# Time mixing on one Trainium2 core: three GpSimd products on VectorE, and the layer norm of batches 1 to 3 on ScalarE

## What is computed

```python
x = x + _time_mixing(_layernorm(x))
x = x + _ffn(_layernorm(x))
```

```python
p = jnp.maximum(pp, u + k);   e1, e2 = jnp.exp(pp - p), jnp.exp(u + k - p)
y = (e1 * aa + e2 * v) / (e1 * bb + e2)
p2 = jnp.maximum(pp + w, k);  e1, e2 = jnp.exp(pp + w - p2), jnp.exp(k - p2)
aa, bb, pp = e1 * aa + e2 * v, e1 * bb + e2, p2
out = (sigmoid(r) * y) @ W_out.T
```

## Time and profile before

| what | value |
|---|---|
| runs, median of 3 (lowest, highest) | 1751.03 us (1748.39, 1753.09) |
| the profiled execution's own time | 1743.46 us |
| its span, first to last instruction | 1741.7 us |
| busy in the span: PE, DVE, ACT, POOL | 92%, 83%, 64%, 61% |
| mean granted TensorE clock | 0.973 |

### The profile page before, as it was taken

How to read it: one execution, slowest core, us unless ns; L and a number is a source line. 1 busy time by engine, 2 the same in 40 slices (tenths; PEclk the granted TensorE clock), 3 DMA queues, 4 the chain that set the end, 5 groups by cost and what they waited for, 6 DMA issues and landing times.

```text
span 1741.7 us, 75944 instructions
## 1 busy us (share of the span) xinstructions
PE 1595.3 (92%) x32157; PEld 1274.2 (73%) x32157; DVE 1448.0 (83%) x3173; ACT 1116.3 (64%) x2014; POOL 1070.8 (61%) x1040
## 2 busy tenths in 40 slices
PE   5469999999999999999999999999999999999985
PEld 2247877777877777777777777777787777877863
DVE  8979988888888888879888888888889888888851
ACT  4346666676676666667667666666666666766652
POOL 3556766756766666666665766566567476575530
PEclk7689999999999999999999999999999999999997
DMA  2011110211110201111211111211111211011010
GB/s 85 31 44 48 40 49 24 76 37 35 44 49 24 76 24 48 43 36 37 60 40 48 31 49 32 59 35 50 41 36 40 61 36 48 26 46 52 28 42 13
DMA packets 41079, 74.97 MB, mean 43 GB/s; under 512 B 9472, under 2 KB 22568, under 8 KB 40744
## 3 DMA queue, kind: packets, MB, share of 16 engines
q1 hardware_dynamic: 40744, 70.12, 13.9%
HBM read 20.08 MB, written 2.10 MB: 13 GB/s over the span
## 4 chain that ended last, share of the span: by engine, by line
PE 73%; issue 9%; DVE 7%; ACT 4%; POOL 3%; ACTq 0%; DVEq 0%; POOLq 0%
PE bank L1350 8%; PE bank L1384 8%; PE bank L1453 8%; PE bank L1319 8%; PE wide L1424 7%; PE bank L1321 6%; PE bank L1320 6%; PE bank L1439 4%; PE bank L1508 4%; PE bank L1402 3%; PE bank L1374 2%; PE bank L1496 2%; PE bank L1498 2%; PE bank L1497 2%; POOL qk L847 1%
## 5 line engine op out<-in xcount | busy, mean ns | idle before, releaser
L855 POOL TENSOR_TENSOR qk<-qk,rnorm 128x512 f32<-128x512 f32 x384 | 401.7, 1046 | 347.8 <-DVE rnorm L1008 347.8
L847 POOL TENSOR_TENSOR qk<-qk,qk_sin 128x512 f32<-128x512 f32 x384 | 492.4, 1282 | 174.4 <-DVE qk_sin L969 174.3
L1171 ACT ACTIVATE squares<-bank 128x512 f32<-128x512 f32 x384 | 229.5, 598 | 154.0 <-DVE qk_sin L969 153.9
L979 DVE TENSOR_REDUCE norm<-squares 128x8 f32<-128x512 f32 x384 | 258.5, 678 | 30.7 <-ACT squares L1171 28.5
L1319 PE MATMUL bank<-w_hi,xs_hi 128*128 128x512 f32 x576 | 262.5, 456 | 13.0 <-ACT squares L1171 6.8
L962 DVE TENSOR_TENSOR qk<-bank,tables 128x512 f32<-128x512 f32 x384 | 261.7, 681 | 8.9 <-PE bank L1321 8.6
L969 DVE TENSOR_TENSOR qk_sin<-bank,tables 128x512 f32<-128x512 f32 x384 | 261.2, 680 | 0.6 <-POOL qk L847 0.6
L1321 PE MATMUL bank<-w_hi,xs_lo 128*128 128x512 f32 x576 | 229.6, 399 | 0.0
L1350 PE MATMUL bank<-ident,qk 128*128 128x128 f32 x1536 | 226.7, 278 | 2.8 <-POOL qk L855 1.7
L1320 PE MATMUL bank<-w_lo,xs_hi 128*128 128x512 f32 x576 | 228.4, 396 | 0.0
L1350 PEld LDWEIGHTS bank<-ident,qk 128*128 128x128 f32 x1536 | 180.9, 142 | 42.0 <-issue 2.8
(11 more groups left out here) (177 smaller groups left out, 2749.1 us busy)
## 6 DMA issues: line engine op xcount, KB each, us to landing
v<-v SPq DMA_DIRECT2D x96, 390.0 KB, 3.5
v<-v SPq DMA_DIRECT2D x72, 130.0 KB, 3.6
w_raw<-in_L_ffn_Wqkv SPq DMA_DIRECT2D x36, 256.0 KB, 3.8
w_o_s<-in_L_ffn_Wo SPq DMA_DIRECT2D x6, 512.0 KB, 5.9
w_raw<-in_L_ffn_W SPq DMA_DIRECT2D x6, 341.0 KB, 4.7
mix_x_nat<-in_L_attn_x SPq DMA_DIRECT2D x4, 256.0 KB, 3.5
w_raw<-x_res_scratch SPq DMA_DIRECT2D x4, 256.0 KB, 4.0
out<-w_raw SPq DMA_DIRECT2D x4, 256.0 KB, 3.3
```

The costliest lines, as they stand in the source:

```text
L847: pool.tensor_tensor(qk[:, g % 2, c, :], qk[:, g % 2, c, :], qk_sin[:, (QK_CHUNKS * g + c) % SINES, :], ALU.add).then_inc(added[c], 1)
L855: pool.tensor_tensor(view, view, rnorm[:, g % 2, c * HPC:(c + 1) * HPC].unsqueeze(2) .to_broadcast([P, HPC, DH]), ALU.mult).then_inc(norme ...
L979: dve.tensor_reduce(norm2[:, c * HPC:(c + 1) * HPC], squares[:, c % 2, :].rearrange("p (h d) -> p h d", d=DH), AX.X, ALU.add).then_inc(sum ...
```

## The change

`numerator` leaves POOL. Its three operations stand in DVE's `weigh_output`, between the operations that were there, so that no operation follows directly on the one it depends on. POOL's loop now waits for the finished denominator of batch b (den2_ready), then splits chunk 2 + b, then does newton(b - 1). The layer norm of batches 1 to 3 leaves DVE: DVE makes one more small tile, offset = -mean * rstd (128x12), and ACT writes xn as rstd * x + offset, four operations of 128x128 for a batch, with both factors read per partition from SBUF. That of batch 1 stands behind exponentials(0), that of b + 2 at the head of ACT's loop. Batch 0's stays on DVE.

```diff
-            def numerator(b):
...
             for b in range(BATCH):
-                numerator(b)
+                pool.wait_ge(den2_ready, b + 1)
                 weights.split(pool, 0, 2 + b)
                 newton(b - 1)
...
                 dve.wait_ge(f2_ready, b + 1)
+                dve.wait_ge(v_evac, b + 1)
+                dve.tensor_tensor(f2v[:], f2[:, p], v_s[:, p], ALU.mult).then_inc(f2v_ready, 1)
                 dve.wait_ge(f1b_ready, b + 1)
                 dve.tensor_tensor(den[:], f1b[:], f2[:, p], ALU.add).then_inc(den_ready, 1)
+                dve.wait_ge(aa_ready, b + 1)
+                dve.tensor_tensor(f1a[:], f1[:, p], aa[:, p, 0:SEQ], ALU.mult).then_inc(f1a_ready, 1)
                 dve.wait_ge(er_ready, b + 1)
                 dve.wait_ge(den_ready, b + 1)
                 dve.scalar_tensor_tensor(den[:], er[:, p], 1.0, den[:], ALU.add, ALU.mult).then_inc(den2_ready, 1)
+                dve.wait_ge(f1a_ready, b + 1)
+                dve.wait_ge(f2v_ready, b + 1)
+                dve.tensor_tensor(num[:], f1a[:], f2v[:], ALU.add).then_inc(num_ready, 1)
...
             spread(NBLK, BATCH * NBLK)
-            layer_norm(1)
+            dve.scalar_tensor_tensor(offset[:, NBLK:], mv[:, NBLK:, 0], -1.0, rstd[:, NBLK:], ALU.mult,
+                                     ALU.mult).then_inc(xn_ready, 1)
             for b in range(BATCH):
...
                 scan_maximum(b + 1)
-                layer_norm(b + 2)
                 weigh_output(b)
...
+            def layer_norm(b):
+                if not real(b):
+                    return
+                act.wait_ge(xn_ready, NBLK + 1)
+                for j in range(b * NBLK, (b + 1) * NBLK):
+                    act.activation(xn[:, j, :], x_nat[:, j, :], ACT.Identity, bias=offset[:, j:j + 1],
+                                   scale=rstd[:, j:j + 1]).then_inc(xn_ready, 1)
...
             exponentials(0)
+            layer_norm(1)
             take_x(1)
...
             for b in range(BATCH):
+                layer_norm(b + 2)
                 take_centred(b - 1)
```

More of the change, by code:

```diff
@@ L223, in time_mixing @@
         var, rstd, root_s, root_w = (sb(name, [P, BATCH * NBLK]) for name in ("var", "rstd", "root_s", "root_w"))
+        offset = sb("offset", [P, BATCH * NBLK])
         var2, rstd2, nt2 = (sb(name, [P, 2, NBLK]) for name in ("var2", "rstd2", "nt2"))
@@ L321, in newton @@
                 pool.tensor_tensor(y, s, y, ALU.mult).then_inc(rs_ready, 1)
-            def numerator(b):
-                p = b % 2
-                pool.wait_ge(f2_ready, b + 1)
-                pool.wait_ge(v_evac, b + 1)
-                pool.tensor_tensor(f2v[:], f2[:, p], v_s[:, p], ALU.mult).then_inc(f2v_ready, 1)
-                pool.wait_ge(f1_ready, b + 1)
-                pool.wait_ge(aa_ready, b + 1)
-                pool.tensor_tensor(f1a[:], f1[:, p], aa[:, p, 0:SEQ], ALU.mult).then_inc(f1a_ready, 1)
-                pool.wait_ge(f1a_ready, b + 1)
-                pool.wait_ge(f2v_ready, b + 1)
-                need(pool, rwkv_ready, b)
-                pool.tensor_tensor(num[:], f1a[:], f2v[:], ALU.add).then_inc(num_ready, 1)
             for c in range(2):
@@ L378, in layer_norm @@
             def layer_norm(b):
-                if not real(b):
-                    return
                 for j in range(b * NBLK, (b + 1) * NBLK):
@@ L580, in turn_x @@
                     return
-                pe.wait_ge(xn_ready, 4 * b + 4)
+                pe.wait_ge(xn_ready, NBLK * (b + 1) + (b > 0))
                 need(pe, xt_evac, 2 * b - 1)
```

## The result

| | kernel before | changed kernel |
|---|---|---|
| median of 6 runs each, us | 1750.47 (1748.39 to 1758.67) | 1740.32 (1738.88 to 1746.60) |
| ratio to before, 95% interval | | 0.9942 [0.9917, 0.9967] |
| profiled execution, us | 1743.46 | 1739.93 |
| its span, us | 1741.7 | 1737.8 |
| first DVE operation of the second block | 87.23 | 84.74 |

The median is 0.58% lower, outside the predicted range of 1743.5 to 1754. The first block ended 2.49 us earlier (forecast: 1.96). The median fell by 10.15 us, four times that. So there are two questions: where the 2.5 us came from, and where the rest did.

A forecast was written before the change was run, and what follows sets the result against it. DVE's queue was taken to bound turns 1 and 2, ACT and PE the start of turn 1, other engines the end. Terms +1.54, -1.57, -2.12, -0.84, +1.03 sum to -1.96: 1751.03 to 1749.0 us, range 1743.5 to 1754.

The forecast's parts named there:

- the base: Whole kernel: the difference is added to the median of the runs, 1751.03 us, not to the profiled execution, 1743.46.
- the sum: First block: +1.54 - 1.57 - 2.12 - 0.84 + 1.03 = -1.96 us.
- signs of being wrong: residual(0) before 42, scale_state waiting for the widening in turns 2 or 3, or second block's length moving over a microsecond.
- The second block starts that much earlier and is the same code: Second block: starts 1.96 us earlier with unchanged code, so the whole kernel gains that much.
- Start to residual(0): Block's start up to residual(0): ACT's four operations ahead of exponentials(1) cost 1.68, factors come 0.14 earlier; 1.54 us later.
- ACT's price: Rival, ACT's new layer-norm operations: 0.72 apart instead of 0.42 gives 1751.5, chance 0.10; 0.16 apart gives 1747.0, chance 0.05.
- The rival on PE's clock: Batch 2's projections: earlier transposes find PE at full level, path up to 3.15 us shorter, 1745.9; chance 0.15.
- Turns 1 to 3: residual(0) to batch 1's reciprocal -1.57; reciprocal to residual, batches 1 and 2, -2.12; residual(1) to batch 2's reciprocal -0.84.
- I cost it at nothing; the spare half microsecond is the cover: Reciprocal to residual: late newton plus widening take about 7.5 us, done before scale_state some 8 us behind num; no cost.
- The end: residual(2) to the block's end: newton follows the split at 6.85 instead of 5.82; 1.03 us later.
- The interleaving hides nothing: Rival, weigh_output's six operations: 0.78 apart like dependent ones, turns 1 to 3 pay 3.24, total 1752.3; chance 0.08.
- e2v: DVE product between reciprocal and residual, blocked by POOL's f2v: 1.75 us falls to 0.69, 1.06 less, twice.

The follow-up runs named there:

- newton first: Against the changed kernel, POOL's last turn runs newton(2) ahead of the wait and the split; 1739.11 us (1 run), second block at 82.83.
- layer norm alone: Against the kernel before, only the layer norm of batches 1 to 3 moves to ACT, products stay on POOL; 1743.61 us, ratio 0.9993.
- split at once: Against the changed kernel, POOL's wait for the denominator is removed; 1736.34 us (1 run), second block at 87.12.
- in a row: Against the changed kernel, weigh_output's six operations reordered so num, den and den2 directly follow what they need; 1751.81 us (1 run).

## Why the prediction was wrong, and where it was right

**The step that failed is the base, not the sum.** The prediction saw that the profiled execution "lies 7.57 us, 0.43%, under the median of the runs, 1751.03", and said "so I add the difference to the median". It took the scatter of three runs, "2.6 below and 2.1 above", as that of the kernel. Later runs of the same code had medians of 1742.72 and 1743.98 with single ones from 1734.65 to 1753.39. Against the profiled execution it had written 1741.5; the changed kernel's profiled execution took 1739.93. What made the six first runs of before so high stays open: all lie at 1748.39 or above, and of the 89 later ones of the same code only 17 do, too few for all of six to be ordinary scatter. The three later groups ran on three chips (14, 6 and 12), and for the first comparison the record names none, so that a difference of the chip is neither shown nor excluded. The profiled execution was none of the six.

**The sum, -1.96 against -2.49, is near partly by luck.** Its first term came out 2.06 us better than forecast and its last 1.17 worse, and the two largely cancel; only the terms in between were sized right. All three of the prediction's signs of being wrong came: residual(0) before 42 (41.75), scalings that wait in turns 2 and 3, and a second block 1.4 us off.

**"The second block starts that much earlier and is the same code"** is half right. It starts earlier in all three profiles of the changed kernel (2.49, 2.82 and 2.49 us, each against the profile of before taken beside it). That it takes as long as before is true at most on average. The prediction's sign of failure, a second block that moves by more than a microsecond, is one that the unchanged kernel shows by itself (1654.5, 1653.9, 1649.8).

**Start to residual(0): forecast +1.54, measured -0.52.** The mechanism held: ACT's extra operations delay the exponentials and everything behind. The sizes did not:

- ACT's price of 0.42 came out at 0.39; 0.12 on four operations. The figure from the Trainium skill (ScalarE: Activation LUTs, What ACT_TABLE_LOAD costs), 0.39, is what the rows show.
- The layer norm of batch 1 ends at 21.83 where 22.10 was forecast: 0.27.
- PE's clock gave the rest. The projections of batch 1 passed to the 2.4 GHz level earlier (1.46 and 1.02 us where before had 1.92 and 1.19), about 0.6; those of batch 2 and the output product likewise, 0.65 + 0.45 = 1.10. The rival on PE's clock had up to 3.15 us, on the projections of batch 2 alone, at a chance of 0.15; there 0.65 came, and 1.05 more on the output product and on batch 1, which it had not named. Its condition was met, and did not do what it said: the earlier transposes ran at the full level (four in 0.63 us, 1.09 before), but PE then idled for 3.52 us, and the first projection was back at 2.07. Nothing here shows that this is owed to the change: the repeat of the changed kernel has the last projection at 1.02, the third profile at 1.48, and two later profiles of before have residual(0) at 41.71 and 41.80 with no wait at all, so that the changed kernel's profiles taken beside them have it 0.53 earlier and 0.07 later. In those two, POOL took the lead away again: the scan of the maximum, beside POOL's f1a, lasts 1.82 us, 1.21 in the changed kernel.

**Turns 1 to 3: forecast -1.57, -2.12 and -0.84; measured -1.51, -2.09 and -0.57.** This was the core of the argument and it stands: DVE operations drawn out by POOL regain their length, independent operations stand 0.60 apart. The 0.27 missed in the third stretch is mostly the wait for the widening in turn 2 (0.16) and xd and yd, 0.67 apart instead of 0.60. "I cost it at nothing; the spare half microsecond is the cover" was too bold: the scaling waits 0.16 in turn 2 and 0.62 in turn 3, 0.46 of it by PE's clock.

**The end: forecast +1.03, measured +1.86 to the last scaling and +2.20 to the second block.** The cause is the one named, newton behind the split (shown by newton first). Missing were the wait of the scaling ahead of it (0.62, of which 0.52 reached newton's start), one operation of newton held by rwkv (0.32), and 0.34 between the last scaling and the next block. That gap is 0.98 us in all six profiles in which the split waits for den2 and newton comes last, 0.64 or 0.65 in before, layer norm alone and split at once; what it consists of is not shown.

**The rivals.** *The interleaving hides nothing* fell: 0.60 apart as written, 0.72 to 0.80 in a row. The Trainium skill (VectorE: DVE Perf Modes, The DRAIN you can't avoid) says that an operation begins when the pipe is empty and that chaining without semaphores gains nothing. No run here leaves a semaphore out, so the second half stands untested; of the first, the rows show that what stands ahead matters: an operation follows a needed one of 0.69 us after 0.72 to 0.80, an unneeded one after 0.60. *ACT's price* was decided at 0.39, far from the 0.67 at which the sum would turn; yet, with the products on DVE, the layer norm's move was worth nothing for another reason, that what it took off DVE came back at residual(0).

What stays open: the difference of the totals. The first block's 2.5 us is shown in three pairs of profiles; that the totals differ by 0.15% accordingly isn't shown, and the first ratio, 0.9942, isn't explained by anything in the traces, beyond the base that did not come back.

## What to carry to other kernels

Look first at how far the time of unchanged code scatters between sets of runs; a copy of the kernel timed against itself shows it, and a sum of 2 us on 1740 is then best read from the position of a marker in the trace. When two engines take turns with each other, move the work of the less critical one to where the other runs an operation that takes no part (here the reciprocal), and put independent operations between dependent ones. Work taken off a busy engine is worth only what the chain behind it lets through: a queue freed ahead of a wait waits longer.

## What the runs showed that I had not expected

- The second block, the same instructions throughout, took 1647.4 to 1662.6 us in 14 profiles, and identical kernels timed together differed by 0.24% with an interval that left out 1.
- An operation on 12 columns of 0.17 us is held to the end of POOL's operation of 1.27 us and lasts 1.12, 0.95 more; the e2v on 512 columns paid 1.06: the small ones pay almost as much.
- The time of a run goes with its granted TensorE clock: 0.001 less is about 1.2 us more, within sets of runs of one kernel.
- PE's step to its upper level comes at a different projection from one profile to the next of the same kernel: the third projection of batch 2 took 1.27, 1.02 and 1.48 us in three profiles of the changed kernel.
